# Loads of the totals issued at the end of the first block, and tile 0 taken ahead of tile 1 with one semaphore for each bias

## The chip, the cores and the metric

The kernel runs on one core of a Trainium2 chip. The metric is the device time of one execution in microseconds (us). The core has five engines that run their own instruction streams and meet at semaphores: PE (TensorE, matmuls; its weight loads are shown as PEld), DVE (VectorE), ACT (ScalarE), POOL (GpSimd) and SP (SyncE, which mostly issues DMAs). SP, ACT and POOL issue DMAs; SP's and ACT's go over hardware queues, POOL's over a software queue, and 16 DMA engines move the bytes of all of them.

## What is computed

A graph of 3327 nodes (padded to 3328 = 26 tiles of 128) with 256 features goes through two layers. Each layer is `x = x + attention(layernorm(x), adj)` and then `x = x + moe(layernorm(x))`, where the mixture of experts sends each node to the best two of eight experts:

```python
x = x + _L0_gnn_ref(_layernorm(x), adj, W, r)
x = x + _L0_ffn_ref(_layernorm(x)[None], gate_w, gate_b, W1, b1, W2, b2)[0]   # top 2 of 8, hidden 512
x = x + _L1_gnn_ref(_layernorm(x), adj, ...)
x = x + _L1_ffn_ref(_layernorm(x)[None], Wr, br, ln_g, ln_b, W1, b1, W2, b2)[0]  # top 2 of 8, hidden 1024

# an expert, for the nodes that chose it, y added into the node's row with its weight
h = gelu(xe @ W1[e] + b1[e]);  y = h @ W2[e] + b2[e]
```

## The kernel before

The program is cut into blocks. At the end of a block every engine runs a DRAIN instruction and they all meet (the rows show it under the block's line). Block 1 (line 2502) holds layer 0, attention `A0` and experts `X0`; block 2 (line 2568) holds layer 1, attention `A1`/`Q1` and experts `X1`. Between them stand `clear_and_free_semaphores` (line 2558, run by POOL) and `all_engine_barrier` (line 2559).

**The experts' tiles.** Routing sorts the node-expert pairs into 59 slots of 128 rows, each of one expert. For slot g, POOL gathers 128 rows from `xs` (L2274), ACT normalizes them (`norm`, L2376 and L2378, the second gives `rx_ready`), PE turns them (`turn_x`, L2315, gives `tx_ready`), ACT copies the turned tile out (`keep_x`; a plain copy L2363 in layer 0, in layer 1 two ACTIVATEs L2367 behind a register load of the expert's number; gives `xgt_ready`), PE multiplies by W1 (`hidden`, L2308, 16 matmul records in layer 0, 32 in layer 1, gives `h_ready`), ACT adds b1 and applies gelu (L2400, gives `ht_ready`), PE multiplies by W2 (L2347, gives `y_ready`), DVE adds b2 and scales (L2427, L2430), and POOL adds the rows by an indirect DMA into a total (L2296, counted by `added`). SP loads the expert's W1 for each slot into one of two buffers (`load_w1`, L2234 and L2235). In steady state PE runs hidden(g+1), turn_x(g+2), W2(g), one behind another.

**Their start.** SP waits for `tiles_known`, loads W1 of tile 0, in layer 0 also b1, then W1 of tile 1 and b2 (L2244: every expert's b2 spread over 128 partitions, 1 MB). In layer 1, b1 is loaded earlier, at L1983. b1 and b2 count on one semaphore, `b_loaded`; ACT waits for 32 (both) before its first gelu and DVE before its first add. PE's order is turn_x(0), turn_x(1), hidden(0), then in `tile(0, 0)` hidden(1), turn_x(2), W2(0). ACT's is norm(0), norm(1), keep_x(0), keep_x(1), norm(2), the wait for the biases, gelu(0).

**The boundary.** In layer 0 even slots are added into `xd` and odd ones into `xe`. POOL ends block 1 by waiting for the last of them. Block 2 starts with `A1.back_load`: SP loads `xd` into `X` in four pieces (2, 3, 4 and 4 pairs of tiles: 512, 768, 1024 and 1024 KB, in rows of 1 KB), ACT loads the first piece of `xe` into `other` and POOL the other three (all L484). Behind these SP gives the starting ones of the block's semaphores (`give_ones`, L2479), and POOL adds two bias vectors (L590). DVE waits for that add, sets a column of V (L517), and then goes piece by piece (`pieces_vector`): for each pair `X += other` (L497) and two statistics (L501), at the piece's end the norm (`norm_of`, up to L506), and only behind the norm of piece 1 the first two `keep` adds (L514, give `pp_free`). ACT normalizes the tiles (L563); PE turns them (L703) and multiplies twice (L713, L716), the products of pair 1 only when `keep` of pair 0 has freed their bank.

Of the kernel before, what the change touches and what calls it, by code (L numbers as in the profile page):

```python
# [40 lines left out]
P = 128  # L41
NODES = 3327
T = 26
NP = T * P
D = 256
# [57 lines left out]
def program(nc, x_in, adjT, w0T, w0, r0, w1, w1T, uv1, proj_wT, bias1, proj_b1,  # L103
# [3 lines left out]
    with ctx:  # L107
# [142 lines left out]
        class SecondWeights:  # L250
# [4 lines left out]
            def __init__(self):  # L255
                self.w_cols = 4 * L1.HD + 2 * 4
                k = WORK_AT
                self.wmat = words(k, KC * self.w_cols)
                k += KC * self.w_cols
                self.proj = words(k, KC * D)  # L260
                k += KC * D
                self.attn_vec = words(k, KC * 8)
                k += KC * 8
                self.bias = words(k, D)
                k += D
                self.gate_in = words(k, KC * E)
# [11 lines left out]
                self.vectors_copied = nc.alloc_semaphore(name="second_vectors_copied")  # L278

            def turned_sync(self, sp):  # L280
# [54 lines left out]
        class Attention:  # L335
            def __init__(self, L, tag):
# [19 lines left out]
                if H > 1:  # L356
                    self.conv = [words(k + s * NP // 2, NP // 2).bitcast(BF16) for s in range(2)]
                    self.other = words(k, T * D)
# [51 lines left out]
                self.center_ready = sem(tag + "center_ready") if H == 1 else None  # L410
                self.xd_back = [sem(f"{tag}xd_back{c}") for c in range(4 * (H > 1))]
                self.xe_back = [sem(f"{tag}xe_back{c}") for c in range(4 * (H > 1))]
                self.norm_known = sem(tag + "norm_known")
                self.far_known = sem(tag + "far_known")
                self.x_whole = sem(tag + "x_whole")
                self.stat = sem(tag + "stat")
# [10 lines left out]
                self.reach_ready = sem(tag + "reach_ready")  # L427
                self.far_steps = sem(tag + "far_steps")
                self.own_turned = sem(tag + "own_turned")
                self.own_copied = sem(tag + "own_copied")  # L430
                self.own_stored = sem(tag + "own_stored")
                self.pb = sem(tag + "pb")
# [21 lines left out]
                self.q_stored = sem(tag + "q_stored")  # L454
                self.conv_done = [sem(f"{tag}conv_done{s}") for s in range(2)]
                self.conv_used = [sem(f"{tag}conv_used{s}") for s in range(2)]
                self.rows_loaded = [sem(f"{tag}rows_loaded{s}") for s in range(2)]
# [18 lines left out]

            PIECES = (0, 2, 5, 9, PAIRS)

            def back_load(self, eng, which, first, last):

                to, of, landed = ((X, xd, self.xd_back), (self.other, xe, self.xe_back))[which]
                for c in range(first, last):
                    a, b = 2 * self.PIECES[c], 2 * self.PIECES[c + 1]
                    eng.dma_start(to[:, a * D:b * D].rearrange("p (t d) -> p t d", d=D),  # L484
                                  of[a * P:b * P, :].rearrange("(t p) d -> p t d", p=P)).then_inc(landed[c], 16)

# [1326 lines left out]
        class Experts:  # L1813
            def __init__(self, hidden, tag, weights_at, scratch_at, turned_at, turn_banks, second_norm):
# [130 lines left out]
                self.w1_loaded = [sem(f"{tag}w1_loaded{s}") for s in range(2)]  # L1945
                self.b_loaded = sem(tag + "b_loaded")
                self.w2_loaded = sem(tag + "w2_loaded")
# [17 lines left out]
            def route_sync(self, sp, rows_final, b1m, w2m, total, ln):  # L1965
# [15 lines left out]
                if self.second_norm:  # L1981
                    sp.wait_ge(self.lg_done, T)
                    sp.dma_start(self.b1, b1m).then_inc(self.b_loaded, 16)  # L1983

# [245 lines left out]
            def tiles_sync(self, sp, w1m, b1m, b2m, next_weights=None):  # L2230
# [8 lines left out]
                if not self.second_norm:  # L2239
                    sp.dma_start(self.b1, b1m).then_inc(self.b_loaded, 16)  # L2240
                sp.wait_ge(self.rx_loaded[0], 16)
                load_w1(1, 1)
                sp.wait_ge(self.rx_loaded[1], 16)
                sp.dma_start(self.b2, b2m.partition_broadcast(P)).then_inc(self.b_loaded, 16)  # L2244

# [56 lines left out]
            def tiles_tensor(self, pe):  # L2302
# [16 lines left out]
                pe.wait_ge(self.rx_ready, 1)  # L2319
                turn_x(0)  # L2320
                pe.wait_ge(self.rx_ready, 2)
                pe.wait_ge(self.xgt_ready[0], 2)
                turn_x(1)
                pe.wait_ge(self.w1_loaded[0], 16)
                hidden(0)
                pe.wait_ge(self.tiles_known, 1)
# [31 lines left out]
            def tiles_scalar(self, a):  # L2358
# [22 lines left out]
                a.wait_ge(self.slots_ready, 1)  # L2381
                for g in range(2):
                    norm(g, g, 1)
                a.wait_ge(self.tiles_known, 1)
                if self.second_norm:
                    a.wait_ge(self.lng_loaded, 32)
                for s in range(2):
                    a.wait_ge(self.tx_ready[s], 2)
                    keep_x(s, s)
                norm(2, 2, 1)  # L2390
                a.wait_ge(self.b_loaded, 32)

# [23 lines left out]
            def tiles_vector(self, v):  # L2416

                v.wait_ge(self.tiles_known, 1)
                v.wait_ge(self.b_loaded, 32)

# [81 lines left out]
        with nc.Block() as block:  # L2502
            @block.sync
            def _(sp):
# [7 lines left out]
                X0.route_sync(sp, None, m0b1, m0w2, xd, None)  # L2512
                X0.tiles_sync(sp, m0w1, m0b1, m0b2, second)

            @block.gpsimd
            def _(pool):
# [8 lines left out]
                pool.wait_ge(spare_clean, 64)  # L2525
                X0.tiles_gpsimd(pool, [xd, xe], (A0.x_kept, 16 * PAIRS))

            @block.vector
# [11 lines left out]
            @block.scalar  # L2540
            def _(a):
                A0.values_scalar(a)
                A0.first_rows_scalar(a)
                A0.single_scalar(a)
                X0.route_scalar(a, A0.last_gelu_scalar)
                X0.tiles_scalar(a)

            @block.tensor
# [19 lines left out]
        with nc.Block() as block:  # L2568
            @block.sync
            def _(sp):  # L2570
                A1.back_load(sp, 0, 0, 4)
                give_ones(sp, a1_ones + q1_ones + x1_ones)
# [12 lines left out]
            def _(pool):  # L2585
                A1.back_load(pool, 1, 1, 4)
                A1.pieces_gpsimd(pool)
# [21 lines left out]
            def _(a):  # L2609
                A1.back_load(a, 1, 0, 1)  # L2610
                A1.pieces_scalar(a, Q1)
# [93 lines left out]
```

## Time and profile before

| | us |
|---|---|
| median of 3 runs | 1764.57 |
| lowest and highest | 1763.18, 1766.04 |
| the profiled execution | 1763.65 |
| its span | 1761.9 |

| engine | busy us | share of the span |
|---|---|---|
| PE | 1642.5 | 93% |
| PEld | 1517.5 | 86% |
| ACT | 1019.0 | 58% |
| DVE | 903.2 | 51% |
| POOL | 356.7 | 20% |

Times in rows are microseconds from the span's start. "idle before <-X" says how long the engine had nothing to do and what released it. The granted clock of PE is given as a share of 2.4 GHz: 1.00 is the upper level, 0.50 the lower (1.2 GHz), and a value between them is a stretch in which it changed. The times of the span that the change touches are three: 470 to 485 (start of X0's tiles), 705 to 735 (the boundary), and 1319 to 1334 (start of X1's tiles).

### The profile page before, as it was taken

How to read it: one execution, taken by the hardware profiler on the slowest of the kernel's cores; microseconds unless marked ns; L12 is line 12 of the kernel's file. 1: busy time of each engine (PE TensorE's matmuls, PEld its weight loads, DVE VectorE, ACT ScalarE, POOL GpSimd, SP SyncE). 2: the span in 40 equal slices, each digit the busy share in tenths (PEclk: the TensorE clock that was granted, in tenths of full speed). 3: DMA queues.
4: the chain of work that ended last, by engine and by line, in shares of the span. 5: the costliest groups of instructions: out<-in, count | busy, mean ns of one | idle time of the engine just before them, and what ended most of it. 6: DMA issues, size and time to landing. Idle time of an engine off the chain costs nothing.

```text
span 1761.9 us, 41250 instructions
## 1 busy us (share of the span) xinstructions
PE 1642.5 (93%) x13276; PEld 1517.5 (86%) x13277; DVE 903.2 (51%) x2158; ACT 1019.0 (58%) x2334; POOL 356.7 (20%) x318
## 2 busy tenths in 40 slices
PE   4799999999799999489999999999989999999997
PEld 3678878888699999379999999999978999999997
DVE  4578868877512212468888878877750111111111
ACT  1143444445355555368989999899734555545443
POOL 2110000000166665320000000000012333333332
PEclk9889999999999999799999999999999999999999
DMA  9990000023478887400000000000366666666663
GB/s 161 107 171 21 1 19 9 9 89 127 123 191 213 225 211 179 161 8 20 13 16 19 9 19 13 15 20 12 130 249 216 185 183 183 179 179 179 179 180 94
DMA packets 93536, 190.33 MB, mean 108 GB/s; under 512 B 20777, under 2 KB 67625, under 8 KB 84617
## 3 DMA queue, kind: packets, MB, share of 16 engines
q1 hardware_dynamic: 60745, 139.50, 24.2%
q0 software_dynamic: 31360, 48.69, 17.5%
q10 hardware_dynamic: 1344, 1.05, 0.2%
q8 instruction: 46, 0.75, 0.2%
q14 instruction: 41, 0.34, 0.1%
HBM read 189.22 MB, written 33.22 MB: 126 GB/s over the span
## 4 chain that ended last, share of the span: by engine, by line
PE 52%; DVE 3%; DMA 2%; issue 1%; ACT 1%; POOL 0%; ACTq 0%; DVEq 0%; SPq 0%; POOLq 0%
PE bank L1783 24%; PE bank L2308 12%; PE bank L2347 11%; PE bank L713 1%; PE bank L716 1%; DMA X<-xd 1%; ACT arena L1485 1%; PE bank L2315 1%; DMA X<-m1b 0%; DVE arena L1621 0%; PE bank L2185 0%; DVE arena L1619 0%; PE bank L703 0%; DMA arena<-xs,slot_row 0%; PE bank L2192 0%
## 5 line engine op out<-in xcount | busy, mean ns | idle before, releaser
L1783 PE MATMUL bank<-arena 128*128 128x195 bf16 x5408 | 466.5, 247 | 13.5 <-DVE arena L1621 10.9
L1783 PEld LDWEIGHTS bank<-arena 128*128 128x128 fp8e4 x5408 | 463.2, 97 | 16.8 <-issue 15.8
L1485 ACT ACTIVATE arena<-arena,m_row 128x512 fp8e5<-128x512 f32 (+1 forms) x672 | 401.5, 678 | 43.8 <-DVE arena L1621 31.1
L2308 PEld LDWEIGHTS bank<-X,arena 128*128 128x128 f32 x2832 | 336.6, 194 | 9.9 <-issue 2.9
L2427 DVE TENSOR_TENSOR arena<-bank,X 128x256 f32<-128x256 f32 x118 | 50.1, 425 | 566.4 <-PE bank L2347 563.2
L2308 PE MATMUL bank<-X,arena 128*128 128x128 f32 x2832 | 339.5, 277 | 0.5 <-DMA arena<-m0w 0.4
L2347 PE MATMUL bank<-arena,X 128*128 x1416 | 325.0, 379 | 4.0 <-ACT X L2400 4.0
L1325 PE MATMUL bank<-arena 128*128 (+1 forms) x1352 | 313.3, 387 | 15.1 <-DVE arena L1231 15.0
L1325 PEld LDWEIGHTS bank<-arena 128*128 128x128 f32 x1352 | 253.3, 192 | 56.0 <-issue 20.9
L2347 PEld LDWEIGHTS bank<-arena,X 128*128 128x128 f32 x1416 | 259.9, 190 | 35.0 <-issue 4.4
L1183 ACT ACTIVATE bank<-arena,s_all 128x384 f32<-128x384 f32 (+1 forms) x234 | 133.7, 573 | 186.1 <-DVE arena L1223 184.3
L2400 ACT ACTIVATE X<-bank,arena 128x128 f32<-128x128 f32 x708 | 194.7, 378 | 20.9 <-issue 14.2
L1223 DVE SCALAR_TENSOR_TENSOR arena<-arena,d_all,bank 128x384 f32<-128x384 f32 (+1 forms) x234 | 139.0, 595 | 68.2 <-PE bank L1325 67.1
L2223 POOL IOTA arena<- 128x118 bf16 x2 | 1.6, 778 | 824.3 <-PE bank L2185 824.3
L2367 ACT ACTIVATE X<-bank,arena 128x128 f32<-128x128 f32 x118 | 47.6, 454 | 201.3 <-PE bank L2315 201.3
L2296 POOL DMA_INDIRECT out<-X,slot_row x59 | 93.4, 1583 | 270.9 <-DVE X L2430 267.8
L1619 DVE SCALAR_TENSOR_TENSOR arena<-arena 128x512 uint32<-128x512 uint32 (+1 forms) x168 | 109.6, 652 | 73.0 <-PE bank L1783 53.4
L2274 POOL DMA_INDIRECT arena<-xs,slot_row x118 | 116.6, 988 | 98.0 <-DVE slot_row L2132 59.6
L1231 DVE TENSOR_TENSOR arena<-arena 128x384 f32<-128x384 f32 (+1 forms) x234 | 125.0, 537 | 0.0
L1621 DVE SCALAR_TENSOR_TENSOR arena<-arena 128x512 uint32<-128x512 uint32 (+1 forms) x168 | 108.8, 648 | 0.0
L2363 ACT COPY X<-bank 128x256 f32<-128x256 f32 x59 | 22.0, 372 | 88.1 <-PE bank L2315 88.1
L2378 ACT ACTIVATE arena<-arena 128x256 f32<-128x256 f32 x118 | 69.7, 590 | 0.0
(250 smaller groups left out, 1359.6 us busy)
## 6 DMA issues: line engine op xcount, KB each, us to landing
arena<-m1w SPq DMA_DIRECT2D x67, 1024.0 KB, 13.3
arena<-m0w SPq DMA_DIRECT2D x67, 512.0 KB, 7.6
arena<-qd SPq DMA_DIRECT2D x25, 256.0 KB, 3.1
arena<-adjT POOLq DMA_DIRECT2D x13, 448.0 KB, 12.9
arena<-adjT POOLq DMA_DIRECT2D x13, 384.0 KB, 10.8
xs<-X SPq DMA_DIRECT2D x14, 256.0 KB, 2.6
xe<-zeros POOLq DMA_DIRECT2D x1, 3456.0 KB, 21.6
X<-x_in SPq DMA_DIRECT2D x2, 1664.0 KB, 11.8
```

Of the source, the lines that this page charges most:

```text
L1183: a.activation(self.exp_bank[s][:, 0:nt * P], self.rows[r][:, 0:nt * P], ACT.Exp, bias=s_all[:, at(c, 1)]).then_inc(self.exp_ready[s], 1)
L1223: v.scalar_tensor_tensor(out=self.prob[q][:, 0:w], in0=self.rows[r][:, W:W + w], scalar=d_all[:, at(c, 1)], in1=self.exp_bank[s][:, 0:w], ...
L1231: v.tensor_tensor(self.prob[q][:, 0:w], self.prob[q][:, 0:w], mask[:, at(c * NP + b * W, w)], ALU.min).then_inc(self.prob_ready[q], 1)
L1325: last = pe.matmul(bank[3 * r + n][:, 0:D + 1], self.prob[q][:, n * P:(n + 1) * P], V[:, at(c * VW, D + 1)], start=False, stop=False, skip ...
L1485: last = a.activation(self.sign[slot].bitcast(F8W)[:, q * W:q * W + nt * P], self.row[r][:, 0:nt * P], ACT.Sigmoid, scale=STEEP, bias=self ...
L1619: v.scalar_tensor_tensor(out=pos, in0=sg, scalar=1, in1=m, op0=ALU.logical_shift_left, op1=ALU.bitwise_and).then_inc(self.pos_ready, 1)
L1621: v.scalar_tensor_tensor(out=neg, in0=sg, scalar=0x08080808, in1=m, op0=ALU.bitwise_xor, op1=ALU.bitwise_and).then_inc(self.neg_ready[slot ...
L1783: last = pe.matmul(bank[rb * NT + n][:, kind * KW:(kind + 1) * KW], self.split[slot][kind].bitcast(F8)[:, q * W + n * P:q * W + (n + 1) * ...
L2274: pool.indirect_dma_start(self.rx[g % 4], None, xs[:, :], bass.IndirectOffsetOnAxis(ap=slot_row[:, g:g + 1], axis=0)).then_inc(self.rx_loa ...
L2308: last = pe.matmul(bank[2 * s + c // 4][:, c % 4 * P:(c % 4 + 1) * P], self.W1[s][:, k * HID + c * P:k * HID + (c + 1) * P], self.rxt[s][: ...
L2347: last = pe.matmul(bank[5 + s][:, 0:D], self.ht[s][:, c * P:(c + 1) * P], self.W2[:, at(e * (HC * D) + c * D, D)], start=(c == 0), stop=(c ...
L2400: last = a.activation(self.ht[s][:, c * P:(c + 1) * P], bank[2 * s + c // 4][:, c % 4 * P:(c % 4 + 1) * P], ACT.Gelu, bias=self.b1[:, at(e ...
```

## The change

Three edits. First, `back_load` moves from the start of block 2 to the end of block 1, on the same three engines and with the same pieces; each of SP, ACT and POOL first waits until all of X0's additions have landed (`added`). Its eight semaphores and the place of `other` are set up with the second layer's weights, outside of what is cleared between the blocks. Second, the first tile of the experts: PE runs turn_x(0), hidden(0), turn_x(1), and ACT norm(0), keep_x(0), norm(1), keep_x(1), norm(2). Third, b1 and b2 get a semaphore each; ACT waits for b1 alone, DVE for b2 alone. About a dozen semaphores that layer 0 never used are no longer allocated for it.

```diff
+            def back_load(self, eng, which, first, last, added):
+                to, of, landed = ((X, xd, self.xd_back), (self.other, xe, self.xe_back))[which]
+                for s in range(2):
+                    eng.wait_ge(added[s], 16 * (RUN_TILES // 2 + 1 - s))
+                for c in range(first, last):
+                    a, b = 2 * self.PIECES[c], 2 * self.PIECES[c + 1]
+                    eng.dma_start(to[:, a * D:b * D].rearrange("p (t d) -> p t d", d=D),
+                                  of[a * P:b * P, :].rearrange("(t p) d -> p t d", p=P)).then_inc(landed[c], 16)
...
-                sp.dma_start(self.b2, b2m.partition_broadcast(P)).then_inc(self.b_loaded, 16)
+                sp.dma_start(self.b2, b2m.partition_broadcast(P)).then_inc(self.b2_loaded, 16)
...
                 pe.wait_ge(self.rx_ready, 1)
                 turn_x(0)
+                pe.wait_ge(self.w1_loaded[0], 16)
+                pe.wait_ge(self.xgt_ready[0], 2)
+                hidden(0)
                 pe.wait_ge(self.rx_ready, 2)
-                pe.wait_ge(self.xgt_ready[0], 2)
                 turn_x(1)
-                pe.wait_ge(self.w1_loaded[0], 16)
-                hidden(0)
...
-                for g in range(2):
-                    norm(g, g, 1)
+                norm(0, 0, 1)
                 a.wait_ge(self.tiles_known, 1)
                 if self.second_norm:
                     a.wait_ge(self.lng_loaded, 32)
-                for s in range(2):
-                    a.wait_ge(self.tx_ready[s], 2)
-                    keep_x(s, s)
+                a.wait_ge(self.tx_ready[0], 2)
+                keep_x(0, 0)
+                norm(1, 1, 1)
+                a.wait_ge(self.tx_ready[1], 2)
+                keep_x(1, 1)
                 norm(2, 2, 1)
-                a.wait_ge(self.b_loaded, 32)
+                a.wait_ge(self.b1_loaded, 16)
...
-                v.wait_ge(self.b_loaded, 32)
+                v.wait_ge(self.b2_loaded, 16)
...
                 X0.tiles_sync(sp, m0w1, m0b1, m0b2, second)
+                second.back_load(sp, 0, 0, 4, X0.added)
...
                 X0.tiles_gpsimd(pool, [xd, xe], (A0.x_kept, 16 * PAIRS))
+                second.back_load(pool, 1, 1, 4, X0.added)
...
                 X0.tiles_scalar(a)
+                second.back_load(a, 1, 0, 1, X0.added)
...
-                A1.back_load(sp, 0, 0, 4)
...
-                A1.back_load(pool, 1, 1, 4)
...
-                A1.back_load(a, 1, 0, 1)
```

## Rows read from the trace of the kernel before

**Rows 1.** The chain that ended last: start us, us, what.

```profile
713.95 13.40 DMA X<-xd
...
1320.75 8.75 DMA X<-m1b
```

**Rows 2.** Timeline of the start of X0's tiles, 470 to 485.

```profile
470.60 0.36 SPq L2235 DMA_DIRECT2D arena<-m0w  x1
...
472.73 0.44 PE L2315 MATMUL bank<-ident,arena 128*128 128x128 f32 x2 [1.67 <-ACT arena L2378]
...
476.27 5.65 PE L2308 MATMUL bank<-X,arena 128*128 128x128 f32 x32
...
483.68 1.14 ACT L2400 ACTIVATE X<-bank,arena 128x128 f32<-128x128 f32 x4 [6.02 <-issue]
...
484.98 1.99 PE L2347 MATMUL bank<-arena,X 128*128 x8 [2.84 <-ACT X L2400]
```

**Rows 3.** End of block 1, POOL's sequencer at line 2502: duration in ns, start.

```profile
L2502 POOLq DRAIN  x1: 2350/2350/2350, 709.3 to 709.3; - x1
```

**Rows 4.** Timeline of the boundary, 713 to 735: start, us, engine, line, operation.

```profile
713.48 10.49 SPq L484 DMA_DIRECT2D X<-xd  x4
...
713.97 2.75 POOL L484 DMA_DIRECT2D arena<-xe  x3 [7.10 <-POOLq L2559]
...
716.71 0.76 POOL L590 TENSOR_TENSOR arena<-arena 128x256 f32<-128x256 f32 x1
...
719.41 0.69 DVE L497 TENSOR_TENSOR X<-X,arena 128x512 f32<-128x512 f32 x1 [1.64 <-DMA arena<-xe]
...
724.83 1.14 PE L703 MATMUL bank<-ident,arena 128*128 128x128 f32 x4 [18.83 <-ACT arena L563]
...
727.38 0.96 DVE L497 TENSOR_TENSOR X<-X,arena 128x512 f32<-128x512 f32 x1 [3.44 <-DMA X<-xd]
...
733.50 0.75 DVE L514 TENSOR_TENSOR X<-bank,X 128x256 f32<-128x256 f32 x2
...
734.07 1.10 PE L713 MATMUL bank<-arena 128*128 128x256 f32 x4 [2.19 <-DVE X L514]
```

**Rows 5.** Timeline of the start of X1's tiles, 1319 to 1334.

```profile
1319.24 0.44 PE L2315 MATMUL bank<-ident,arena 128*128 128x128 f32 x2 [1.24 <-ACT arena L2378]
...
1322.83 8.95 PE L2308 MATMUL bank<-X,arena 128*128 128x128 f32 x64
...
1323.77 0.81 ACT L2367 ACTIVATE X<-bank,arena 128x128 f32<-128x128 f32 x2 [1.33 <-PE bank L2315]
...
1330.79 2.18 ACT L2400 ACTIVATE X<-bank,arena 128x128 f32<-128x128 f32 x8 [5.44 <-issue]
...
1333.12 3.72 PE L2347 MATMUL bank<-arena,X 128*128 x16 [1.12 <-ACT X L2400]
```

**Rows 6.** Short windows: us, busy of each engine, then PEclk, DMA share, GB/s.

```profile
1323.00:1323.50 0.50, 0.50 (x6) 0.50 (x6) 0.00 (x0) 0.00 (x0) 0.23 (x1) 0.88 0.94 393
...
480.00:480.50 0.50, 0.50 (x5) 0.50 (x5) 0.00 (x0) 0.00 (x0) 0.00 (x0) 0.72 0.66 272
...
1326.50:1327.00 0.50, 0.50 (x5) 0.50 (x5) 0.00 (x0) 0.00 (x0) 0.00 (x0) 0.71 1.08 459
...
729.00:730.00 1.00, 1.00 (x6) 0.71 (x6) 0.97 (x3) 0.28 (x2) 0.00 (x0) 0.77 1.08 378
```

**Rows 7.** Line 484's own issues on SP: duration in ns, min/median/max.

```profile
L484 SPq DMA_DIRECT2D X<-xd x4: 412/517/8899, 713.5 to 715.1; - x4
```

**Rows 8.** End of the opening block (line 2481), SP's sequencer: duration in ns.

```profile
L2481 SPq DRAIN  x1: 7/7/7, 3.1 to 3.1; - x1
```

**Rows 9.** SP's two loads of x (line 182): issue, and time to landing.

```profile
L182 SPq DMA_DIRECT2D X<-x_in x2: 456/703/950, 0.8 to 1.3; - x2
...
DMA to landing us min/median/max: 9.6/11.8/14.0
```

**Rows 10.** POOL's last two loads of xe: KB, median us from issue to landing.

```profile
arena<-xe POOLq DMA_DIRECT2D x2, 1024.0 KB, 12.4
```

More of the change, by code:

```diff
@@ L278, in __init__ @@
                 self.vectors_copied = nc.alloc_semaphore(name="second_vectors_copied")
+                self.other = words(k + 4 * D, T * D)
+                self.xd_back = [nc.alloc_semaphore(name=f"second_xd_back{c}") for c in range(4)]
+                self.xe_back = [nc.alloc_semaphore(name=f"second_xe_back{c}") for c in range(4)]
+            PIECES = (0, 2, 5, 9, PAIRS)
+            def back_load(self, eng, which, first, last, added):
[6 more added lines that the diff above has]
+                                  of[a * P:b * P, :].rearrange("(t p) d -> p t d", p=P)).then_inc(landed[c], 16)
             def turned_sync(self, sp):
@@ L357, in __init__ @@
                     self.conv = [words(k + s * NP // 2, NP // 2).bitcast(BF16) for s in range(2)]
-                    self.other = words(k, T * D)
+                    self.other = second.other
                     other_end = k + T * D
@@ L410, in __init__ @@
                 self.center_ready = sem(tag + "center_ready") if H == 1 else None
[L411 to L415, printed above, removed]
+                self.xd_back, self.xe_back = second.xd_back, second.xe_back
+                self.norm_known = sem(tag + "norm_known") if H > 1 else None
+                self.far_known = sem(tag + "far_known") if H > 1 else None
+                self.x_whole = sem(tag + "x_whole") if H > 1 else None
                 self.stat = sem(tag + "stat")
@@ L427, in __init__ @@
                 self.reach_ready = sem(tag + "reach_ready")
[L428 to L431, printed above, removed]
+                self.far_steps = sem(tag + "far_steps") if H > 1 else None
+                self.own_turned = sem(tag + "own_turned") if H > 1 else None
+                self.own_copied = sem(tag + "own_copied") if H > 1 else None
+                self.own_stored = sem(tag + "own_stored") if H > 1 else None
                 self.pb = sem(tag + "pb")
@@ L454, in __init__ @@
                 self.q_stored = sem(tag + "q_stored")
-                self.conv_done = [sem(f"{tag}conv_done{s}") for s in range(2)]
-                self.conv_used = [sem(f"{tag}conv_used{s}") for s in range(2)]
+                self.conv_done = [sem(f"{tag}conv_done{s}") for s in range(2 * (H > 1))]
+                self.conv_used = [sem(f"{tag}conv_used{s}") for s in range(2 * (H > 1))]
                 self.rows_loaded = [sem(f"{tag}rows_loaded{s}") for s in range(2)]
@@ L474, in __init__ @@
                                     + self.rows_free + self.exp_used + self.prob_used + self.banks_free + [self.acc_free])
[L477 to L485, printed above, removed]
+            PIECES = SecondWeights.PIECES
             def pieces_vector(self, v, Q):
@@ L1945, in __init__ @@
                 self.w1_loaded = [sem(f"{tag}w1_loaded{s}") for s in range(2)]
-                self.b_loaded = sem(tag + "b_loaded")
+                self.b1_loaded = sem(tag + "b1_loaded")
+                self.b2_loaded = sem(tag + "b2_loaded")
                 self.w2_loaded = sem(tag + "w2_loaded")
@@ L1982, in route_sync @@
                     sp.wait_ge(self.lg_done, T)
-                    sp.dma_start(self.b1, b1m).then_inc(self.b_loaded, 16)
+                    sp.dma_start(self.b1, b1m).then_inc(self.b1_loaded, 16)
             def route_vector(self, v, x_stored):
@@ L2239, in tiles_sync @@
                 if not self.second_norm:
-                    sp.dma_start(self.b1, b1m).then_inc(self.b_loaded, 16)
+                    sp.dma_start(self.b1, b1m).then_inc(self.b1_loaded, 16)
                 sp.wait_ge(self.rx_loaded[0], 16)
```

## The prediction

> **What bounds the kernel now.** I read the page first: PE is busy 93% of the span, so an edit that takes no PE work away can only win in the few holes of PE. Then the chain that ended last, to see which holes have a wait on the path. It is almost all PE matmuls; of the places that the change touches it names two transfers, the load of `xd` at the boundary (13.40 us) and the load of b2 in X1 (8.75 us) [rows 1]. Last the timelines of the three stretches, and for each the row where PE starts again and what released it. The reader is to see three things there. In X0, W2 of tile 0 starts at 484.98, released by ACT's gelu, which had been idle for 6.02 us before 483.68 while hidden(0) and hidden(1) ran from 476.27 to 481.92 [rows 2]. At the boundary, POOL has left its last wait just before its drain at 709.3 [rows 3], the loads start at 713.48, DVE's first add is at 719.41, its next piece waits 3.44 us for `xd` and starts at 727.38, and PE stands still for 2.19 us until 734.07 for the `keep` behind that piece [rows 4]. In X1, W2 of tile 0 starts at 1333.12, again behind a gelu, but only 1.12 us after PE's last work [rows 5].
>
> Behind each of the three places PE works one tile after another, so a shift of PE's restart there reaches the end unchanged: I take W2(0) of X0, the PE row at 734.07, and W2(0) of X1 as the three marks, and each term below is the shift of one mark.
>
> **Term 1, start of X0.** Removed: ACT's wait for b2. In X1 b2 landed at 1320.75 + 8.75 = 1329.50 [rows 1] and gelu began at 1330.79 [rows 5], 1.29 later (the wait's end, and the register load of the expert's number). So in X0 b2 landed near 483.68 - 1.29 = 482.4, and everything else that W2(0) needs was there by 481.9 to 482.3. Moved: hidden(0) no longer stands behind norm(1) and turn_x(1). turn_x(0) ends at 472.73 + 0.44 = 473.2 [rows 2]; keep_x(0), a copy, takes some 0.4 (half of the two that take 0.81 in X1 [rows 5]), so hidden(0) could start at 473.7 instead of 476.27. It also needs W1 of tile 0, issued at 470.60 [rows 2]. Its landing isn't in the trace: the bounds are 473.7 (then it hides) and 476.2 (it had landed before hidden(0) ran). I take 475.3, nearer the late end, since 512 KB and the gathers beside it need some 4 to 5 us.
>
> How long hidden(0) takes hangs on the clock. In X1 64 records took 8.95 us [rows 5] of which some 3.3 were at the lower level (from its fall within the window at 1323.0 until its rise within the one at 1326.5 [rows 6]); with r for one record at the upper level, 3.3/2r + 5.65/r = 64, r = 0.114 us. So 16 records take 1.8 us at 2.4 GHz and 3.7 at 1.2. In X0 the clock was at 1.2 GHz and rose in the window 480.0 to 480.5 [rows 6], some 4 us after PE had gone back to work. I keep that instant: hidden(0) 475.3 to 479.0. Added: a hole, for turn_x(1), keep_x(1) and hidden(1) now stand behind hidden(0) one after another: 0.5 + 0.1 + 0.4 + 0.1, to 480.1. hidden(1) at the upper level ends at 482.0, turn_x(2) at 482.4, W2(0) starts at 482.5. ACT is done before that: b1 was issued with W1 and is small, ACT reaches its wait near 479.9, gelu starts 1.3 later and takes 1.14. DVE's b2 is needed only when W2(0) ends, at 484.5, after 482.4. Gain 484.98 - 482.5 = **2.5 us**; bounds 3.3 (W1 at 473.7) and 0.5 (W1 at 476.2 and the clock 1.5 us later). W1 of tile 2 is issued when hidden(0) ends, 1 us earlier than before, and needed 2.5 us earlier; I count no wait there, for b2, which stands in front of it in SP's queue, is no later than before.
>
> **Term 2, the boundary.** Moved: 8 DMA issues, four on SP, one on ACT, three on POOL, and they are moved in front of the block's end. They can start when POOL's wait ended, 709.15, against 713.48: 4.35 us earlier [rows 3, 4]. Added: a wait for `added` on SP and ACT, which have nothing left to do. But every engine behind the barrier now also waits for the issuing itself. SP's four issues took 10.49 us, the fourth alone 8.90 [rows 4, 7]: SP stood in that instruction until 723.97, when part of the earlier pieces had moved. In the kernel before this held up only SP. The same four transfers in front of the same empty queue should hold it again: 709.15 + 10.49 = 719.65, a drain that costs nothing (SP's took 7 ns at 3.1 us with two loads out that landed 9.6 us or more after their issue [rows 8, 9]), and then what lay between POOL's drain (709.3 + 2.35 = 711.65 [rows 3]) and 713.48, 1.83 us. Block 2 starts at about **721.6 instead of 713.48**. POOL's side is shorter: three issues 2.75 [rows 4], drain 2.35, to 714.3.
>
> From there: POOL's bias add 0.76 [rows 4] and the column of V, so DVE's first add is at 723.1 instead of 719.41, 3.7 late, but with piece 0 landed and piece 1 about to (713.95 + 13.40 = 727.35 [rows 1], less 4.35 = 723.0). DVE needs 719.41 to 727.38 - 3.44 = 723.94, 4.53, for piece 0 [rows 4] and starts piece 1 at 727.65 instead of 727.38, so the wait of 3.44 is gone and nothing is won by it: `keep` is at 733.8. PE's first turn comes some 3.5 later than 724.83 (it had waited a little for SP's ones, held behind the fourth load, which is over), and its work up to 734.07 - 2.19 = 731.88 ends at 735.4. PE had a hole of 2.19 there, which takes most of it up: the mark moves from 734.07 to 735.4, **1.4 us later**. This term lies between two waits, so its bounds are wide: the clock rose some 4.4 us after PE's start there (724.83, window 729 to 730), and about 4 us after hidden(0)'s start in X0 and X1 [rows 6]; a rise 1.5 us sooner or 2.4 later is worth -0.8 or +1.2 us, and instructions of block 2 that must be fetched while the loads run may add up to 1. So -0.2 to +3.5.
>
> [...]
>
> **Term 3, start of X1.** keep_x(0) starts some 0.8 to 0.9 after its turn (hidden(0) follows turn_x(1) at 1322.83, and keep_x(1) starts at 1323.77) and takes 0.81 [rows 5], behind a turn that ends at 1319.24 + 0.44, so hidden(0) could run at 1321.4 instead of 1322.83, if its W1 of 1 MB has landed; it had by 1322.8. I take 1322.4, and the same fall of the clock at 1323.4: then hidden(0) ends 0.4 earlier, at 1327.7 (before: 1328.1, by r). The new hole is larger here: turn 0.4, 0.8 for the register load, 0.81, 0.1, together 2.1 us, in which PE does nothing and which hidden(0) used to cover. hidden(1) takes 3.65, to 1333.5, turn_x(2) to 1333.8. Before, W2(0) started 1.12 after PE was free, so the b2 wait was worth only that. Mark: 1333.85 instead of 1333.12, **0.7 us later**. Bounds: -0.4 (W1 there at 1321.4), and +3 if the hole pulls the clock down again for hidden(1); a hole of 2.19 us at 731.9 did not.
>
> Everything else has one answer: the dozen semaphores fewer shorten the clearing by at most some hundredths, and each engine's own order elsewhere is unchanged.
>
> **Sum.** -2.5 + 1.4 + 0.7 = -0.4 us. Against the profiled execution, 1763.65 (span 1761.9 and 1.75 around it), that is 1763.3. That run lies 0.9 below the median, to which I add the same difference: 1764.57 - 0.4 = 1764.2.
>
> **Rivals.** (a) *SP is not held at the fourth load*, or only briefly, at the end of block 1. For it: it is a transfer that the hardware takes over, and three of the four issues took about half a microsecond. Against: the 8.90 us. Then POOL ends last, at 714.3, block 2 starts at 716.2, the first add is at 717.5 (1.9 early), piece 1 lands at 723.0, `keep` comes at 729.2 and PE's work of piece 0 ends at 731.88 - 1.9 = 730.0: the mark moves 4.1 earlier. Sum -2.5 - 4.1 + 0.7 = -5.9, time 1758.7. (b) *POOL's drain waits for its own loads.* This ends on the slow side. For it: the drain took 2.35 us behind indirect DMAs although these had landed, so it does something with that queue, and no row shows one with loads out. Against: SP's drain didn't wait. POOL's last two 1 MB loads took 12.4 us in the middle [rows 10], the last about 13.5; issued at 711.1 it would land at 724.6, block 2 would start at 726.4, the first add at 727.9, 8.5 late, and the mark moves by 8.3 - 2.2 = 6.1. Sum -2.5 + 6.1 + 0.7 = +4.3, time 1768.9. It is slower than before from the point where the drain ends after about 722. (c) *Tile 0 wins nothing*: W1 lands late and the clock rises later in X0, so that term 1 is 0.5 and term 3 is up to 3: sum -0.5 + 1.4 + 1.5 to 3, +2.4 to +3.9, time 1767.7.
>
> **How the numbers follow.** Forecast (within 1761.5 to 1767): 0.58. (a) 0.18, (b) 0.12, (c) 0.12. A measurement of this kernel can tell some 0.2%, 3.5 us, from no change. Faster by more than that, under 1761.0: all of (a) and a little of the forecast's best ends, 0.23. Slower, over 1768.1: (b) and a third of (c), and upper bounds together, 0.18. The rest, 0.59, is no difference. The range takes in (a)'s time and (b)'s: 1758.6 to 1769.0. The forecast's own range is 1761.5 to 1767.
>
> **What would show it.** In the timeline of the changed kernel: SP's fourth issue at L484 still some 9 us long and now in front of the drain of line 2502 of block 1; the start of block 2 (POOL's L590) 12 us after the loads' start rather than 7; no wait of DVE's L497 on `xd`; the hole of PE before the first L713 of pair 1 gone. At both tile starts: a hole of PE of 1 us (X0) and 2 us (X1) between two groups of L2308, gelu not behind b2, and W2(0) right behind turn_x(2). The prediction is wrong if SP's four issues end together within 2 us, if POOL's drain is longer than 8 us, or if the clock is at the lower level for hidden(1).

## The result, and the profile of the changed kernel

The changed kernel takes 1770.74 us (median of 6, 1768.59 to 1771.77) against 1764.45 for the kernel before beside it (median of 6, 1761.47 to 1766.04): ratio 1.0036, interval 1.0026 to 1.0046. It is slower by some 6.3 us. The forecast was 1764.2 with its own range from 1761.5 to 1767, and the wide range, which took in the rivals, ended at 1769.0. The profiled execution took 1770.75, span 1769.0 (before: 1763.65 and 1761.9). One of e9's ten executions below (2163.58 us) and one of e8's six (1975.64) ran at a granted clock of 0.75 and 0.83; their medians are of all executions, their ratios leave these two out.

Line numbers shift: the loads of line 484 are line 292 now, the adds of line 497 are L503, `keep` is L520, the projection is L719, POOL's add of the bias is L596, and block 1 ends at line 2510. In the tiles the turn is L2322, the hidden products L2315, gelu L2408, W2 L2354.

First the changed kernel's end of block 1. The sequencers' own instructions at line 2510 show duration in ns and start; this is where [rows 3] stood:

```profile
L2510 ACTq DRAIN  x1: 152/152/152, 707.6 to 707.6; - x1
L2510 POOLq DRAIN  x1: 14988/14988/14988, 708.6 to 708.6; - x1
L2510 SPq DRAIN  x1: 123/123/123, 716.5 to 716.5; - x1
```

POOL's drain, 2.35 us before, takes 14.99. SP's and ACT's, with loads out as well, take 0.12 and 0.15. SP's row begins at 716.5 since SP stands in its fourth load until then. POOL is 7.1 us behind it: its drain ends at 723.6, and block 2 starts 2.0 later. The issues themselves, by source line:

```profile
L292 SPq DMA_DIRECT2D X<-xd x4: 407/523/7597, 707.2 to 708.8; - x4
L292 POOL DMA_DIRECT2D arena<-xe x3: 912/920/962, 707.7 to 709.6; - x3
```

The timeline of the changed kernel's boundary (start, us, engine, line, operation, in brackets the idle time and who ended it), the counterpart of [rows 4]:

```profile
703.30 1.54 POOL L2303 DMA_INDIRECT xd<-X,slot_row  x1 [0.30 <-issue]
...
707.21 9.19 SPq L292 DMA_DIRECT2D X<-xd  x4
...
707.73 2.75 POOL L292 DMA_DIRECT2D arena<-xe  x3 [2.88 <-DMA xd<-X,slot_row]
...
725.68 0.72 POOL L596 TENSOR_TENSOR arena<-arena 128x256 f32<-128x256 f32 x1 [15.20 <-POOLq L2570]
...
726.55 0.67 DVE L503 TENSOR_TENSOR X<-X,arena 128x512 f32<-128x512 f32 x1 [0.65 <-issue]
...
731.80 1.13 PE L709 MATMUL bank<-ident,arena 128*128 128x128 f32 x4 [27.82 <-ACT arena L569]
...
740.08 1.10 PE L719 MATMUL bank<-arena 128*128 128x256 f32 x4 [1.54 <-DVE X L520]
```

The reader is to see that POOL is idle for 15.20 us between its third issue and its first add, PE for 27.82. That the drain ends with the landing of POOL's own third load is seen from the view of DMA. For the issues from 706 to 709.9 it gives

```profile
arena<-xe POOLq DMA_DIRECT2D x2, 1024.0 KB, 12.1
```

and for the second of them alone 10.9, so the third took 2 x 12.1 - 10.9 = 13.3. Issued at 709.6, it landed at 722.9, 0.7 us before the drain's end.

The three marks, and what lies between them, from the same rows of every profile (us). "First gather" is the start of the first `DMA_INDIRECT arena<-xs` of X0 or X1, "last scatter" the start of POOL's last `DMA_INDIRECT` into `xd`, "mark" the start of PE's first product of pair 1 (L719). The fourth and fifth columns split the boundary at DVE's first add:

| kernel | X0: first gather to W2(0) | X0: first gather to last scatter | last scatter to first add | first add to mark | mark to X1's first gather | X1: first gather to W2(0) |
|---|---|---|---|---|---|---|
| before | 16.12 | 236.5 | 14.08 | 14.66 | 581.1 | 17.93 |
| after | 10.76 | 234.5 | 23.25 | 13.53 | 581.1 | 19.30 |
| e1_tiles_only | 10.99 | 232.9 | 14.25 | 15.14 | 584.9 | 19.90 |
| e2_loads_only | 16.43 | 238.9 | 23.05 | 14.48 | 581.9 | 18.10 |
| e3_pool_late | 10.60 | 236.4 | 14.43 | 13.63 | 581.2 | 19.31 |
| e4_pool_one | 13.60 | 235.2 | 17.17 | 13.99 | 583.5 | 19.92 |
| e5_three_one | 12.71 | 234.3 | 12.18 | 14.18 | 581.6 | 19.30 |
| e6_split_only | 13.13 | 235.2 | 14.16 | 14.51 | 583.8 | 16.31 |
| e9_l0_order | 10.95 | 233.2 | 14.13 | 14.96 | 585.2 | 17.86 |
| e8_best | 10.82 | 233.0 | 8.90 | 14.57 | 582.0 | 17.15 |
| e10_b2_behind | 10.90 | 234.6 | 9.10 | 13.83 | 581.5 | 17.16 |
| e11_best_again | 10.56 | 234.0 | 9.20 | 13.69 | 581.2 | 17.22 |

From W2(0) of X1 to the end every kernel takes 428.5 to 428.9. After against before: -2.0 for X0, +9.2 and -1.1 at the boundary, +1.4 in X1, together +7.4 (unrounded); the two spans differ by 7.1, the medians of six by 6.3. Each row of the table is one execution. The stretch in the sixth column varies by 4 us although its code is the same, so the times of whole runs blur what the columns show. In e1 and e9 1.7 of it has a place: PE's hole before the mark is 2.78 and 2.64 us there, the clock falls to 0.50 about 1 us behind it, and PE's third group of L719 starts 5.70 after the mark, against 4.02 before.

### The profile page after: what moved, and what is told of

Read it like the earlier page. It is cut to its first block, busy times and chain, and to the rows that moved or that the text cites. A ratio compares the mean times of both kernels' runs of the same rounds, so it can differ in the third digit from the quotient of the medians.

```text
span 1769.0 us, 41249 instructions
## 1 busy us (share of the span) xinstructions
PE 1641.2 (93%) x13276; PEld 1515.7 (86%) x13277; DVE 902.9 (51%) x2158; ACT 1018.6 (58%) x2334; POOL 356.6 (20%) x318
## 4 chain that ended last, share of the span: by engine, by line
PE 52%; DVE 3%; ACT 1%; issue 1%; DMA 1%; POOL 0%; ACTq 0%; DVEq 0%; SPq 0%; POOLq 0%
PE bank L1789 24%; PE bank L2315 12%; PE bank L2354 11%; PE bank L719 1%; PE bank L722 1%; PE bank L2322 1%; ACT arena L1491 1%; DVE arena L1627 0%; PE bank L2192 0%; PE bank L709 0%; DVE arena L1625 0%; DMA arena<-m1w 0%; PE bank L2199 0%; PE bank L2182 0%; DVE arena L1646 0%
## 5 line engine op out<-in xcount | busy, mean ns | idle before, releaser
L1789 PE MATMUL bank<-arena 128*128 128x195 bf16 x5408 | 466.5, 248 | 13.5 <-DVE arena L1627 10.8
L2315 PEld LDWEIGHTS bank<-X,arena 128*128 128x128 f32 x2832 | 335.0, 193 | 21.5 <-issue 7.2
L2315 PE MATMUL bank<-X,arena 128*128 128x128 f32 x2832 | 338.8, 277 | 10.4 <-DMA arena<-m0w 5.0
L2354 PE MATMUL bank<-arena,X 128*128 x1416 | 324.9, 379 | 0.0
L2354 PEld LDWEIGHTS bank<-arena,X 128*128 128x128 f32 x1416 | 260.2, 190 | 30.3
L2408 ACT ACTIVATE X<-bank,arena 128x128 f32<-128x128 f32 x708 | 194.1, 377 | 9.7 <-PE bank L2315 5.1
```

What stands on the lines that cost most here:

```text
L1789: last = pe.matmul(bank[rb * NT + n][:, kind * KW:(kind + 1) * KW], self.split[slot][kind].bitcast(F8)[:, q * W + n * P:q * W + (n + 1) * ...
L2315: last = pe.matmul(bank[2 * s + c // 4][:, c % 4 * P:(c % 4 + 1) * P], self.W1[s][:, k * HID + c * P:k * HID + (c + 1) * P], self.rxt[s][: ...
L2354: last = pe.matmul(bank[5 + s][:, 0:D], self.ht[s][:, c * P:(c + 1) * P], self.W2[:, at(e * (HC * D) + c * D, D)], start=(c == 0), stop=(c ...
L2408: last = a.activation(self.ht[s][:, c * P:(c + 1) * P], bank[2 * s + c // 4][:, c % 4 * P:(c % 4 + 1) * P], ACT.Gelu, bias=self.b1[:, at(e ...
```

## Experiments

Diffs are condensed: repeated lines, and the waits that move with them, are left out. They are against the changed kernel unless another is named. "Before" is the kernel before in the executions beside each run. A given ratio can differ from the quotient of the two medians by up to 0.0008. Where loads go back into block 2 they have no wait.

**e1_tiles_only and e2_loads_only: the two halves of the change, each alone.**

```diff
 e1                                  # block 1's end
-second.back_load(sp, 0, 0, 4, X0.added)
-second.back_load(pool, 1, 1, 4, X0.added)
-second.back_load(a, 1, 0, 1, X0.added)
                                     # block 2's start
+second.back_load(sp, 0, 0, 4, None)
+second.back_load(pool, 1, 1, 4, None)
+second.back_load(a, 1, 0, 1, None)
 e2
-turn_x(0); hidden(0); turn_x(1)
+turn_x(0); turn_x(1); hidden(0)     # and ACT's norms and copies as before
+a.wait_ge(self.b2_loaded, 16)
+v.wait_ge(self.b1_loaded, 16)
```

> Only the edits of the first tiles are kept (order of tile 0, a semaphore for each bias); the loads of the totals stand at the start of block 2 again. Theory (the loss lies in the moved loads): W2(0) of X0 some 5.4 us earlier but 2.0 us kept at the last scatter of X0, W2(0) of X1 1.4 us later against the first gather, boundary as before (28.7 us from the last scatter of X0 to PE's first product of pair 1). Time 0.6 us under before, so within 0.2%. Rival (the tiles' order costs, through the larger hole in X1 or later W1 loads in both loops): 2 us or more above before.

> Only the loads of the totals are moved to the end of block 1; order and waits of the first tiles are those of before. Theory (POOL's DRAIN waits for its own loads): drain about 15 us, 36.8 us from the last scatter to the first product of pair 1 instead of 28.7, time 8 us over before (about 1772.5). Rival (the two edits work against each other in some shared resource, so that the loads alone cost less): time under 1770.

Measured: e1 1762.59 against 1763.81, ratio 0.9990 (0.9980 to 1.0000); e2 1771.71, ratio 1.0041 (1.0027 to 1.0054). The loss is in the loads: e2 alone loses 7.9. The drain of e2's block 1, at line 2511, with the old order of the tiles:

```profile
L2511 POOLq DRAIN  x1: 14754/14754/14754, 711.2 to 711.2; - x1
```

Its third load, by the same working as above, took 13.1 and landed at 725.3, again 0.7 before the drain's end (725.95). The tiles' half doesn't lose; its gain isn't told from nothing by this run.

**e3_pool_late: POOL's three loads go back to block 2, SP's four and ACT's one stay in front of the block's end.** This parts the two suspects, SP's hold at the fourth load and POOL's drain.

```diff
-second.back_load(pool, 1, 1, 4, X0.added)   # block 1's end
+second.back_load(pool, 1, 1, 4, None)       # block 2's start
```

> As the changed kernel, but POOL issues its three loads at the start of block 2, as before; SP's four and ACT's one stay at the end of block 1. Theory (POOL's DRAIN waits for the loads that POOL itself issued): drain 2.4 us; then SP's held fourth load, 9 us, is what ends last, block 2 starts about 12 us after the loads' start (16.5 in the changed kernel), time 2 to 3 us over before less 0.6, about 1766. Rival A (the drain waits for whatever DMA is in flight): drain 13 to 16 us again, block 2 as late as in the changed kernel, time at or over 1770. Rival B (SP's hold does not keep the barrier up): block 2 starts 5 us after the loads' start, time under 1763.

Measured: 1762.23 against 1763.81, ratio 0.9987 (0.9978 to 0.9996); first add 14.43 after the last scatter. Its line 2510, and SP's issues:

```profile
L2510 POOLq DRAIN  x1: 2350/2350/2350, 708.9 to 708.9; - x1
L2510 SPq DRAIN  x1: 123/123/123, 713.4 to 713.4; - x1
...
L292 SPq DMA_DIRECT2D X<-xd x4: 408/522/2928, 708.8 to 710.4; - x4
```

POOL's drain is back at 2.35 us although five loads of other queues are out: it waits for its own. SP is still held, for 2.93 us instead of 7.60, now that POOL's 2.8 MB aren't beside it, and SP is the last at the barrier, at 713.4. So the step of the prediction that SP's hold keeps the barrier does exist; here it eats up what the earlier issue gives (14.43 against 14.08). The drain is as expected, but the hold was expected at 9 us and the time at about 1766: a second miss on the hold's size. The time is one that rival B had named (under 1763), yet not for its reason, for the hold does keep the barrier up.

**e5_three_one: as e3, and SP issues three of its four loads early, the fourth in block 2.**

```diff
-second.back_load(sp, 0, 0, 4, X0.added)     # block 1's end
+second.back_load(sp, 0, 0, 3, X0.added)
-second.back_load(pool, 1, 1, 4, X0.added)
                                             # block 2's start, behind give_ones
+second.back_load(sp, 0, 3, 4, None)
+second.back_load(pool, 1, 1, 4, None)
```

> As the changed kernel, but at the end of block 1 only SP's first three loads and ACT's one are issued; SP's fourth (behind the starting ones) and POOL's three at the start of block 2. Theory: neither hold nor long drain, block 2 starts 4.3 us after the loads' start as in before, DVE's first add 1.8 us earlier than before, no wait for xd, first product of pair 1 about 2 us earlier; time about 1762, 2.5 us under before. Rival (the drain waits for any DMA in flight): drain over 8 us, time over 1768.

Measured: 1759.75 against 1763.81, ratio 0.9974 (0.9964 to 0.9984). No issue of SP is held (0.38 to 0.55 us each, the fourth at 712.8), SP's drain begins at 706.9, and the first add comes 12.18 after the last scatter. From there to the first product of pair 1 it is 26.36, 2.4 less than before, as expected. What the first add then waits for is not a load:

```profile
709.90 2.75 POOL L292 DMA_DIRECT2D arena<-xe  x3 [6.99 <-POOLq L2569]
...
713.55 0.68 DVE L503 TENSOR_TENSOR X<-X,arena 128x512 f32<-128x512 f32 x1 [3.88 <-issue]
```

POOL first issues its three loads and only then adds the bias that DVE's add needs: 2.75 us in front of everybody, which nothing in the kernel before showed as a cost since the piece wasn't there yet.

**e4_pool_one: one load of POOL, the smallest, stays in front of the block's end**, with ACT's; SP's four and POOL's other two go to block 2.

```diff
-second.back_load(sp, 0, 0, 4, X0.added)     # block 1's end
-second.back_load(pool, 1, 1, 4, X0.added)
+second.back_load(pool, 1, 1, 2, X0.added)
                                             # block 2's start
+second.back_load(sp, 0, 0, 4, None)
+second.back_load(pool, 1, 2, 4, None)
```

> As the changed kernel, but at the end of block 1 POOL issues only its first load (768 KB) beside ACT's one (512 KB); all of SP's and POOL's other two are issued at the start of block 2. Theory (POOL's DRAIN lasts until POOL's own load has landed): the load lands about 5 us after its issue, and the drain ends within 1 us of that landing, so it is 4 to 6 us long. Rival (a drain with any load of POOL's out has a fixed long price, or one that goes by something else): drain near 15 us, or 2.35 us.

Measured: one time, 1767.47 (before beside it 1762.73), so no interval. The drain, and the load that it stands behind, issued at 706.91:

```profile
L2510 POOLq DRAIN  x1: 6942/6942/6942, 706.9 to 706.9; - x1
```

```profile
arena<-xe POOLq DMA_DIRECT2D x1, 768.0 KB, 6.3
```

It landed at 713.2 (expected after about 5 us, it took 6.3), and the drain ends at 713.9, 0.7 later, as with three loads. With none 2.35, with one 6.94, with three 14.99 and 14.75: the drain's end follows the landing of POOL's last load, which settles the cause. SP's four loads, now in block 2 with POOL's other two beside them:

```profile
L292 SPq DMA_DIRECT2D X<-xd x4: 411/518/1803, 715.6 to 717.2; - x4
...
716.36 1.81 POOL L292 DMA_DIRECT2D arena<-xe  x2 [8.53 <-POOLq L2569]
```

The fourth is held for 1.80 us, less than the 2.93 of e3, although 2 MB of POOL's are beside it here and none there.

**e6_split_only: the semaphore of each bias alone, with the old order of the tiles and the loads as before.**

```diff
-turn_x(0); hidden(0); turn_x(1)
+turn_x(0); turn_x(1); hidden(0)
                                     # loads as in e1
```

> Only a semaphore for each bias; loads of the totals and order of the first tiles as in before. Theory: gelu of tile 0 follows hidden(0) and the load of b1; from the first gather to W2(0) X0 13.5 us (before 16.1) and X1 16.9 (before 17.9), boundary as before; time 2 to 3 us under before. Rival (the earlier start runs into the W1 loads queued behind b2 and gives it back): time within 1 us of before.

Measured: 1761.28 against 1762.73, ratio 0.9992 (0.9982 to 1.0002): 1.5 under, where 2 to 3 were expected, and not told from nothing. W2(0) in X0 comes at 13.13 instead of 16.12, in X1 at 16.31 instead of 17.93: without the wait for b2 3.0 and 1.6 us less, of which in X1 0.5 is a faster clock in the first 64 records (8.48 against 8.95). The new order takes a further 2.2 off in X0 but adds to X1: the five kernels that have it there lie at 19.30 to 19.92, the five with the old order and two semaphores at 16.31 to 17.86, on the mean 2.4 less.

**e9_l0_order: as e1, with the new order in X0 only.**

```diff
+if self.second_norm:
+    turn_x(0); turn_x(1); hidden(0)
+else:
+    turn_x(0); hidden(0); turn_x(1)
```

> The order of tile 0 is changed in layer 0 alone, a semaphore for each bias in both, loads of the totals as in before. Theory: X0 from the first gather to W2(0) 10.8 us with some 3 us kept at the last scatter, X1 16.9 us; time 3 to 4 us under before. Rival (the new order in X1 was not what cost 1.4 us there): X1 at 19 us again.

Measured: 1760.75 against 1762.73, ratio 0.9981 (0.9971 to 0.9991). This is 2 us under before, where 3 to 4 were expected. X1's start is 17.86, X0's 10.95, so X0 keeps the gain of its new order and X1 no longer pays for one. The expected 16.9 isn't reached in X1, nor e6's 16.31: the same 64 records take 9.98 us here, 8.48 in e6, and 9.2 to 9.4 in e8, e10 and e11 (17.2), so this column spreads by 1.5 with the clock.

**e8_best and e11_best_again: what the others point to.** As e9; SP's first three and ACT's two loads in front of the block's end, none of POOL's; in block 2 SP's fourth behind `give_ones`, and POOL's two behind its add of the bias.

```diff
                                             # against e9, block 1's end
+second.back_load(sp, 0, 0, 3, X0.added)
+second.back_load(a, 1, 0, 2, X0.added)
                                             # block 2
-second.back_load(sp, 0, 0, 4, None)
+second.back_load(sp, 0, 3, 4, None)          # behind give_ones
-second.back_load(pool, 1, 1, 4, None)
-second.back_load(a, 1, 0, 1, None)
-A1.pieces_gpsimd(pool)
+A1.pieces_gpsimd(pool, lambda: second.back_load(pool, 1, 2, 4, None))
```

> A version meant to beat both: at the end of block 1 SP issues its first three loads and ACT its first two of xe, POOL none; in block 2 SP's fourth goes behind the starting ones and POOL's last two behind its bias add; the order of tile 0 is changed in layer 0 alone; a semaphore for each bias. Theory: drain 2.35 us, DVE's first add 2 to 3 us sooner than in the run with three and one, from the last scatter to the first product of pair 1 23 to 24 us (before 28.7), X1 16.9 us; time 8 to 9 us under before. Rival (ACT's second load is held, or the barrier is not what the first add waits for): boundary at 26 us or more, time 5 us under before.

> The version meant to beat both once more, word for word, beside the one with b2 behind W1 of tile 2: the base for that comparison. Expected 8 to 9 us under before, as in its first run (ratio 0.9948), boundary 23.5 us.

Measured: 1754.45 against 1762.73, ratio 0.9948 (0.9935 to 0.9961); again as e11 1753.95 against 1763.40, ratio 0.9945 (0.9931 to 0.9958). It beats both kernels, the one before by 8 to 9 us. Its boundary, first the end of block 1 at its line 2531, then the timeline:

```profile
L2531 POOLq DRAIN  x1: 2350/2350/2350, 705.1 to 705.1; - x1
```

```profile
709.28 0.72 POOL L596 TENSOR_TENSOR arena<-arena 128x256 f32<-128x256 f32 x1 [6.38 <-POOLq L2590]
...
710.09 1.94 POOL L292 DMA_DIRECT2D arena<-xe  x2
...
710.26 0.69 DVE L503 TENSOR_TENSOR X<-X,arena 128x512 f32<-128x512 f32 x1
```

The first add comes 8.90 after the last scatter, 5.2 earlier than before and 3.3 earlier than in e5: 2.75 of these are POOL's issues, which now stand behind the bias; the other 0.5 isn't traced. The mark follows in full, for the first add to the mark takes 14.57 (before 14.66): nothing of the gain is lost to a later load.

**e10_b2_behind: as e8, and in X0 the W1 of tiles 2 and 3 is issued in front of b2.**

```diff
+if next_weights is not None:
+    sp.wait_ge(self.h_ready[0], 2); load_w1(2, 0)
 sp.dma_start(self.b2, ...).then_inc(self.b2_loaded, 16)
+if next_weights is not None:
+    sp.wait_ge(self.h_ready[1], 2); load_w1(3, 1)
```

> As the version meant to beat both, but in layer 0 SP issues b2 behind W1 of tile 2 instead of in front of it. Theory (in the changed kernel and its kin PE waits some 2 us in front of hidden(2) because that W1 stands behind the 1 MB of b2): this wait is under 0.5 us, from W2(0) to PE's next hidden 1.9 us instead of 3.8, DVE's first add starts later but nobody waits for it; time 1 to 2 us under its base. Rival (the DMA engines are simply full then, whatever the order of the queue): the wait stays at about 2 us, or comes back at tile 3 or as a wait for DVE.

Measured: 1754.17 against 1763.40, ratio 0.9943 (0.9930 to 0.9957), no different from e11 beside it; the expected 1 to 2 us under it didn't come. The hole that it is aimed at, first in e11, then in e10 (hidden(2), and in e10 hidden(3) too):

```profile
482.10 2.02 PE L2316 MATMUL bank<-X,arena 128*128 128x128 f32 x16 [2.16 <-DMA arena<-m0w]
```

```profile
481.49 2.02 PE L2322 MATMUL bank<-X,arena 128*128 128x128 f32 x16 [0.21 <-DMA arena<-m0w]
...
485.93 2.05 PE L2322 MATMUL bank<-X,arena 128*128 128x128 f32 x16 [0.47 <-DMA arena<-m0w]
```

The hole of 2.16 is 0.21, a second one of 0.47 takes its place, and the last scatter comes at 234.6 after the first gather against 234.0 in e11. A gain of a microsecond would be lost in the spread of that column (233 to 236 with one order), so what it is worth stays open.

## Why the prediction was wrong

**Term 1, start of X0: right in kind, too small, and then partly given back.** Forecast -2.5 at the mark; the mark came 5.4 earlier (10.76 against 16.12). From hidden(0)'s end to hidden(1)'s start the forecast had 1.1, and it is 1.25. The rows of after:

```profile
474.19 2.05 PE L2315 MATMUL bank<-X,arena 128*128 128x128 f32 x16 [1.10 <-DMA arena<-m0w]
...
477.49 2.02 PE L2315 MATMUL bank<-X,arena 128*128 128x128 f32 x16 [1.03 <-DMA arena<-m0w]
...
479.56 1.89 PE L2354 MATMUL bank<-arena,X 128*128 x8
...
483.62 2.02 PE L2315 MATMUL bank<-X,arena 128*128 128x128 f32 x16 [2.17 <-DMA arena<-m0w]
```

The 1.25 is near the forecast for another reason: what ends it is the landing of W1 of tile 1, which no term had; where that had landed (e9 and e5), PE is idle for only 0.46, until keep_x(1). Two things were mis-sized. W1 of tile 0 lets hidden(0) start 5.4 after the first gather (474.19 - 468.80), where the forecast had 6.4 (475.3). And "I keep that instant" for the clock's rise was wrong: there was no rise, for the clock didn't fall. In a window that reaches into the hole in front of hidden(0), PEclk is 1.00 with PE idle (columns as in [rows 6]):

```profile
473.50:474.00 0.50, 0.00 (x0) 0.00 (x0) 0.00 (x0) 0.05 (x1) 0.20 (x2) 1.00 1.63 340
```

so that 16 records take 2.05 us and not 3.7. This isn't sure to happen: of the nine executions with this order in X0, seven kept 2.4 GHz through hidden(0) and hidden(1) and have W2(0) at 10.6 to 11.0, while in e5 and e4 the clock fell to 1.2, in e5 before hidden(0) and in e4 in the middle of it, and W2(0) came at 12.71 and 13.60; hidden(0) of e5 is

```profile
472.46 3.78 PE L2315 MATMUL bank<-X,arena 128*128 128x128 f32 x16 [1.08 <-DMA arena<-m0w]
```

The step that failed behind it is "I count no wait there" for W1 of tile 2. The last row of after above has a hole of 2.17 us for it: SP issues it only when hidden(0) is done, behind b2, and both are now wanted earlier. With W1 in front of b2 the hole is 0.21 (e10), so b2 is what holds it. Therefore the mark isn't the gain, and the premise that a shift of PE's restart "reaches the end unchanged" doesn't hold in X0: from the first gather to the last scatter after took 2.0 less than before (of the 3.4 lost on the way 2.2 are this hole, the rest isn't traced), and e5, whose W2(0) was 2 late by the clock, finished its tiles no later than after (234.3 and 234.5). Over all executions the stretch is 234.2 on the mean with the new order (eight of them, without e10, 232.9 to 236.4), 236.5 and 238.9 with the old order and one wait, 235.2 with the split alone. So some 3 us are kept, near the forecast 2.5, with a spread as large; that this term came out nearly right is luck, two errors that cancel.

**Term 2, the boundary: the term that made the miss.** Forecast +1.4, measured +8.0 (36.78 against 28.74). The failing step is "POOL's side is shorter: three issues 2.75, drain 2.35". The drain took 15.0, because it waits for the loads that POOL itself has issued. The sum had taken 2.35 from [rows 3], where none was out, and had let SP's drain [rows 8] stand for POOL's. That was rival (b), with a chance of 0.12; e2, e3 and e4 show it. POOL's last load was forecast there to take 13.5 us and took 13.3, but the price was forecast at +6.1 and is +8.0. 0.7 of the difference is the first add, 9.2 late and not 8.5. For the rest the step that failed is that PE's hole of 2.19 "takes most of it up": the stretch from the first add to the mark shrinks by 1.1 only, and the hole itself from 2.19 to 1.54. In the chain of waits of after one sees why:

```profile
738.80 0.27 ACT arena L554
739.07 0.11 ACT rstd L2479
...
739.20 0.20 DVE rstd L2473
...
739.51 0.43 DVE X L520
...
740.08 1.10 PE bank L719 x4
```

`keep` (L520) needs the next piece's norm, whose root on ACT (L2479) stands in ACT's order behind ACT's copies for PE's products (L554), and these follow PE. A late start of PE moves the end of its own hole with it. The hole so has a floor: it is 1.54 to 1.56 us in nine of the twelve traces, and larger only in before, e1 and e9 (2.19, 2.78 and 2.64), where DVE's wait for piece 1 ends it. Of the 2.19 only 0.6 could be taken up.

The step that SP is held at its fourth load, which carried the forecast, was right: 7.60 us, forecast 8.90. It was only not the last: SP was free at 716.5 and POOL at 723.6. With POOL's loads away it is the last (e3), and the first rival (a), in which SP isn't held, was wrong for this edit; e5 makes it true by taking the fourth load away, and then the first add is 1.9 us early, as (a) had it, but the boundary gains 2.4 us, not 4.1, for the same reason of the hole. The Trainium skill (page DMA: Bandwidth & Descriptors, section Anatomy of one DMA, on GpSimd's path) puts the dispatch of such a DMA at some 50 ns. The rows here show 0.91 to 0.96 us for each whole issue of POOL, 2.75 for the three, so they aren't free to whoever stands behind them (e5).

**Term 3, start of X1: right in sign and kind.** Forecast +0.7, measured +1.4 (19.30 against 17.93; 19.3 to 19.9 in the five kernels with this order, and 18.10 in e2 with the old one). The rows of after:

```profile
1328.81 5.88 PE L2315 MATMUL bank<-X,arena 128*128 128x128 f32 x32 [3.30 <-DMA arena<-m1w]
...
1336.56 3.84 PE L2315 MATMUL bank<-X,arena 128*128 128x128 f32 x32 [1.65 <-ACT X L2374]
...
1337.24 2.17 ACT L2408 ACTIVATE X<-bank,arena 128x128 f32<-128x128 f32 x8
...
1340.46 3.62 PE L2354 MATMUL bank<-arena,X 128*128 x16
```

From hidden(0)'s end to hidden(1)'s start it is 1.87, near the 2.1 us of the forecast. The wrong size is hidden(0)'s start: it didn't come 0.4 earlier. In after it waits for W1 of 1 MB and starts 7.65 after the first gather (1328.81 - 1321.16); in before it started at 7.64, right behind turn_x(1), so that W1 had landed by then, and no row shows when. So the new order wins nothing here, and only pays. The forecast's "the b2 wait was worth only" 1.12 was right: of the 1.6 of e6, 0.5 is the clock.

**Sum.** -2.5 + 1.4 + 0.7 was forecast, -2.0 + 8.0 + 1.4 = +7.4 came, so 6.6 of the 7.8 us between them are term 2. Rival (c) had term 3 about right (from 1.5) and term 1 wrong. The range missed since (b) was priced with the hole taking up 2.2; with nothing taken up its end would have been 1771. Two bounds also don't come out of their own steps: term 2's lower one is 1.4 - 0.8 = 0.6 and not -0.2, and term 1's least gain, with W1 at 476.2 and the clock 1.5 later, is some 1.3 and not 0.5. The microsecond for fetching instructions in term 2's bounds is shown by no run. None of this changes the miss. The marks named beforehand did tell: POOL's drain over 8 us.

## What to carry to other kernels

Put loads that are to be in flight across a block's end on queues whose drain doesn't wait for them (here SP and ACT, and only the three that SP issues without being held), and POOL's behind the barrier and behind the small work that others wait for. The row of a drain holds only for what was outstanding when it ran: before a transfer is moved in front of one, look for a row of that engine with a load of its own out, and where there is none, give the wait its full price and a fair chance. A hole absorbs a delay only if what ends it doesn't itself follow the delayed engine, so read the chain that leads into the hole first.

## What the runs showed of the hardware

POOL's drain at a block's end lasts until the loads that POOL issued have landed, and 0.7 us longer (after, e2 and e4): 14.99 and 14.75 us with three out, 6.94 with one, 2.35 with none, whatever other queues have out. SP's and ACT's take 0.12 to 0.15 with theirs in flight.

SP's hold at the fourth load of the `xd` group isn't a fixed price of the instruction: 8.77 to 9.58 us with POOL's three loads and ACT's one beside it in block 2 (before, e1, e6, e9), 7.60 and 6.81 in front of the block's end (after, e2), 2.93 with only ACT's beside it (e3), and none when the fourth comes some 6 us after the third (e5, e8: 0.55 and 0.59 at the most for any of the four). That other queues' bytes set it isn't shown: in e4, where ACT's load and POOL's first had landed but POOL's two of 1 MB were issued beside it, it is 1.80, less than in e3. What sets its length stays open.

In front of hidden(0) of X0, in the nine executions with the new order there, PE stood idle 1.6 to 1.7 us, turned one tile and stood idle 1.0 to 1.8 us more. The granted clock stayed at 2.4 GHz in seven of them and fell to 1.2 in two, which costs up to 1.7 us for 16 records (3.78 against 2.05). The two don't have the longest idle time before hidden(0) (1.08 in e5 and 1.16 in e4; e9, which kept the clock, has 1.77), so these rows alone don't say when it falls.
